# Causal attention between two feed-forward blocks: value products of two units put together in every second step of the attention phase

## The reference, cut to what matters

```
q = x @ w_q.T ; k, v = split(x @ w_kv.T)      # 16 heads of 32, one shared k and v
q, k = rotary(q), rotary(k)
attn = softmax(where(causal, q k^T, -max))     # per head 512 x 512, lower triangle
out  = attn @ v                                # the value product
x    = x + out @ w_proj.T + b_proj
```

## Time and profile before

| | us |
|---|---|
| median of 3 runs | 2837.68 |
| lowest and highest | 2837.28, 2841.86 |
| the profiled execution's own time | 2843.29 |
| its span in the trace | 2841.4 |
| TensorE busy in it | 2738.1 (96%) |
| VectorE, ScalarE, GpSimd busy | 1863.3, 1127.3, 284.3 |
| attention phase in the trace | about 1094 to 1746 |

### The profile page before, as it was taken

The page is one execution under the profiler, slowest core; times in us unless marked ns, Lnnn a source line. Parts: engine busy times, 40 slices in busy tenths (PEclk is TensorE's granted clock), DMA queues, the critical chain, the costliest instruction groups (busy, mean ns, idle before and its releaser), DMA issues. The chain is left out here.

```text
span 2841.4 us, 41676 instructions
## 1 busy us (share of the span) xinstructions
PE 2738.1 (96%) x15520; PEld 2198.9 (77%) x15520; DVE 1863.3 (66%) x3543; ACT 1127.3 (40%) x2400; POOL 284.3 (10%) x295
## 2 busy tenths in 40 slices
PE   7999999999999996899999997999999999999998
PEld 6888888888888884567777765888888888888887
DVE  5667656766676655777777765656766766676655
ACT  3323333323333321677777773332333333333331
POOL 0000000000000002344444421000000000000000
PEclk9999999999999997899999998999999999999999
DMA  3210311121121103000000003211121122203100
GB/s 118 98 51 21 128 45 44 61 89 45 45 78 63 48 4 119 1 9 31 28 28 31 16 16 123 85 45 45 60 89 49 48 79 82 68 17 104 45 15 30
DMA packets 65165, 156.48 MB, mean 55 GB/s; under 512 B 6881, under 2 KB 7137, under 8 KB 64737
## 3 DMA queue, kind: packets, MB, share of 16 engines
q1 hardware_dynamic: 64992, 154.17, 16.1%
HBM read 128.97 MB, written 25.17 MB: 54 GB/s over the span
## 5 line engine op out<-in xcount | busy, mean ns | idle before, releaser
L347 PE MATMUL bank<-xnt_h,wgu_h 128*128 128x512 f32 x2048 | 804.0, 393 | 10.3 <-issue 7.4
L347 PE MATMUL bank<-xnt_h,wgu_l 128*128 128x512 f32 x2048 | 799.4, 390 | 0.0
L347 PE MATMUL bank<-xnt_l,wgu_h 128*128 128x512 f32 x2048 | 799.3, 390 | 0.0
L504 DVE TENSOR_TENSOR h<-bank,sg 128x512 f32<-128x512 f32 x256 | 176.9, 691 | 601.4 <-PE bank L347 587.1
L347 PEld LDWEIGHTS bank<-xnt_h,wgu_h 128*128 128x128 f32 x2048 | 385.9, 188 | 91.8 <-issue 8.9
L347 PEld LDWEIGHTS bank<-xnt_h,wgu_l 128*128 128x128 f32 x2048 | 385.8, 188 | 80.7
L347 PEld LDWEIGHTS bank<-xnt_l,wgu_h 128*128 128x128 f32 x2048 | 386.0, 188 | 79.2
L443 ACT ACTIVATE mag<-h 128x512 f32<-128x512 f32 x256 | 162.2, 634 | 702.5 <-DVE h L504 702.5
L366 PE MATMUL bank<-wd_h,hs_h 128*128 128x512 f32 x1024 | 400.5, 391 | 9.1 <-DVE hs_l L539 9.1
L366 PE MATMUL bank<-wd_l,hs_h 128*128 128x512 f32 x1024 | 399.9, 390 | 0.0
L366 PE MATMUL bank<-wd_h,hs_l 128*128 128x512 f32 x1024 | 399.8, 390 | 0.0
(11 more groups left out here) (107 smaller groups left out, 3060.6 us busy)
## 6 DMA issues: line engine op xcount, KB each, us to landing
raw_gu<-in_w_gu SPq DMA_DIRECT2D x128, 512.0 KB, 4.9
raw_d<-in_w_d SPq DMA_DIRECT2D x128, 256.0 KB, 2.6
x_mid<-x_sb SPq DMA_DIRECT2D x64, 256.0 KB, 2.0
x_sb<-in_x SPq DMA_DIRECT2D x32, 256.0 KB, 4.9
x_sb<-x_mid SPq DMA_DIRECT2D x8, 1024.0 KB, 5.7
x_sb<-x_mid SPq DMA_DIRECT2D x32, 256.0 KB, 4.6
out<-x_sb SPq DMA_DIRECT2D x32, 256.0 KB, 2.1
probs<-in_w_q SPq DMA_DIRECT2D x1, 1024.0 KB, 5.4
```

Of the source, the lines that this page charges most:

```text
L347: last = pe.matmul(ps, w[:, r, kind, k], xs[:, b, k], start=(i == 0), stop=(i == 3 * KD - 1))
L504: v.tensor_tensor(h[:, r], bank[UP + r % 2][:, :], sg[:, r % 2], ALU.mult).then_inc(h_done, 1)
```

## The change

The step of TensorE no longer issues one value product each. Steps of odd row (1 and 3) issue none. Steps of even row issue two: that of unit K - 2 and then that of unit K - 1. So row 0's steps weigh rows 2 and 3 of the head group before, and row 2's steps weigh rows 0 and 1 of their own. After the last step both remaining units are weighed. `pt` keeps its size but is addressed by eight block places: row 0 uses place 7, row 1 places 5 and 6, row 2 places 0, 1 and 2, row 3 places 3, 4, 5 and 6. Nothing else in the program is different: the same matmuls, copies and waits are issued.

```diff
-    pt = place("pt", [P, 2, TT, HG, P], F32)
+    pt = place("pt", [P, 2 * TT, HG, P], F32)
...
+            PLACES = ((7,), (5, 6), (0, 1, 2), (3, 4, 5, 6))
...
                                 last = pe.matmul(outs[s * HD:(s + 1) * HD, i * P:(i + 1) * P], kvtok[:, B % 2, j, 1],
-                                                 pt[:, K % 2, j, s], start=(j == 0), stop=(j == i))
+                                                 pt[:, PLACES[i][j], s], start=(j == 0), stop=(j == i))
...
-                        if K > 0:
+                        if k % 2 == 0 and K > 0:
+                            weigh(K - 2)
                             weigh(K - 1)
                         if K + AHEAD < ALL:
                             scores(K + AHEAD)
...
                     for K in range(ALL):
                         step(K)
+                    weigh(ALL - 2)
                     weigh(ALL - 1)
...
-                        a.copy(pt[:, K % 2, j], bank_of["p", K, j][:, :].rearrange("p (s n) -> p s n", n=P)).then_inc(pt_scalar, 1)
+                        a.copy(pt[:, PLACES[row_of(K)][j]], bank_of["p", K, j][:, :].rearrange("p (s n) -> p s n", n=P)).then_inc(pt_scalar, 1)
...
-                        v.tensor_copy(pt[:, K % 2, j], bank_of["p", K, j][:, :].rearrange("p (s n) -> p s n", n=P)).then_inc(pt_vector, 1)
+                        v.tensor_copy(pt[:, PLACES[row_of(K)][j]], bank_of["p", K, j][:, :].rearrange("p (s n) -> p s n", n=P)).then_inc(pt_vector, 1)
```

## The result

The changed kernel is faster: median 2829.15 us of 7 runs (2826.25 to 2831.38) against 2837.68 before (7 runs, 2834.62 to 2842.28), a ratio of 0.9966 with a 95% interval of 0.9954 to 0.9977, that is 10 us less (7 to 13); the ratio is made from all the runs, and the two medians alone are 8.5 us apart. A second set of runs of the same kernel gave a median of 2828.81 and a ratio of 0.9961 (0.9947 to 0.9975). The forecast was 2820.8, 17 us less. The direction held. The wide range (2815 to 2830) held with 0.85 us to spare; the likeliest case's own range (2816 to 2827) did not hold, and 2829.15 lies in the range that the prediction had given to rival A.

What follows compares the result with a forecast made beforehand. TensorE's own order was taken to set the pace. Visits 8.8, mask waits 9.1 and k = 15 1.3, less 1.4 and 0.9, gave 16.9 us off the median 2837.7: 2820.8, range 2815 to 2830.

Steps and rivals of the forecast that it cites:

- rival A: VectorE's masks late in more steps, so the waits only move; 4 to 9 us saved, say 2831; chance 0.11.
- fewer visits: TensorE's value products: 64 visits instead of 128, 0.14 us saved at each of 63, 8.8 us less.
- Entry to the scores: Odd steps, scores directly behind transposes: priced the same as entry to value products, bounds 0.05 us either way in 63 steps.
- the wait at row 0: Scores S512 waiting for the masks of S384, 0.59 or 0.16 us each: all 9.1 us of waits go.
- k = 15: Batches 0 to 5, a transpose's 1.08 us wait for a bank: 0.22 more work under it, 1.3 us gained.
- list of covers: Check that `pt`, `pv_done`, the exponentials of S512 and ScalarE's slack stay safe with later products; no cost booked.
- the wait at k = 9: Row 1's step without W8: S128 comes 4.87 us after S512, a new wait of 0.03 for masks.
- a sign of being wrong: Odd steps showing scores that wait 0.3 us or more for masks would prove the forecast wrong.
- where VectorE bounds: k = 9, 13 of batch 0 and k = 1, 5 of batch 7: W8's 0.36 us returns nothing, 1.4 lost.
- B: No measurable change: entry to scores and waits inside the pair cost 6 us and A holds too; 2835; chance 0.05.
- C: More saved: entry to scores cheaper by 0.05 us and visits worth more; 21 to 24 us, 2815; chance 0.04.
- D: Slower: a stop makes TensorE's clock fall once per batch, 28 us paid less 17 saved; 2849; chance 0.06.

Runs made afterwards that it cites:

- both waits mended: Changed kernel with row 0's product in its own step at k = 1, 5 (batches 0 to 6), last two statistics at k = 6, 7; 2823.09 us.

## Why the prediction was right or wrong

**Right: fewer visits.** 0.14 for each saved visit, read from W8, W16 and W24, is what joining gave on its own (0.56 for four). Entry to the scores cost the same as entry to the value products, as the rows at the slower clock had it (at k = 1 0.39 us after the turns of k and v begin, with S128 behind them or with W8), and the second product's waits inside a group cost nothing: W56 is 1.67 to the next start, as worked out. The rule of the Trainium skill ("TensorEngine Tiling (Array Packing)", Key Properties), that a change of tiling mode drains the engine, agrees in sign; what a single change costs no run here isolates.

**Right: the wait at row 0.** The 0.59 and 0.16 us are gone, and S384 to S512 is 3.11 as worked out. It was the larger half of the gain: 0.84 of 1.40 with the visits left as they were.

**Right: k = 15.** 1.08 became 0.86, as summed.

**Right in part by luck: the number.** The saving came to 10 us where 17 were forecast, and the range held it because its upper end had been set to take in part of rival A. The step of the prediction that failed most is the next one.

**Wrong: what W8 covered.** The step "fewer visits" put "transposes, S" in place of "transposes, W, S" and priced entry alone. It did not ask which release W8's 0.36 us were hiding. At k = 1 and 5 the projection of a q ends ahead of it, and the bank of that q comes free later, after two operations of VectorE (1.4 us after the projection's end at k = 1). The prediction's list of covers names `pt`, `pv_done`, the exponentials and ScalarE, and leaves out the three banks that go round. It cost 0.26 + 0.23 us in seven batches, 3.4 us in all, the largest miss; the weight loader's two rows of waits above add up to 3.5.

**Wrong in size: the wait at k = 9.** The place and the mechanism were forecast, 0.03 us; it measured 0.27. That is just under the 0.3 that the prediction had named as a sign of being wrong. The working let the scaling of the output begin 0.02 ahead of S512; it begins 0.14 behind it. In the kernel before 0.02 ahead is seen at k = 4, where S512 itself stands waiting and the scaling follows the masks. Where the product's end alone sets it, at k = 0, the kernel before already had 0.13 behind:

```profile
1377.34 1.14 PE L915 MATMUL bank<-kt,qt 32*128 32x512 f32 x8
...
1377.47 0.69 DVE L1175 TENSOR_TENSOR att<-bank,rt 128x512 f32<-128x512 f32 x1 [2.38 <-PE bank L939]
```

The working also took 0.05 from the last mask to the next scores, where 0.14 was seen. In five batches the two are 1.2 us.

**Wrong, the other way: where VectorE bounds.** 1.4 us were booked as lost in batches 0 and 7, because row 2 was to pay for the block that row 1 gained nothing from. In batch 7 at the full clock the two orders end within 0.14 us (43.68 and 43.82). Here are row 2's step with rows 0 and 1 apart, and then the same step with them joined and both waits mended:

```profile
1665.31 0.50 PE L916 MATMUL bank<-kt,qt 32*128 32x128 f32 x8 [1.97 <-DVE nmax L1164]
...
1668.04 0.71 PE L916 MATMUL bank<-kt,qt 32*128 32x256 f32 x8 [0.19 <-DVE nmax L1164]
...
1662.80 0.50 PE L916 MATMUL bank<-kt,qt 32*128 32x128 f32 x8 [2.32 <-DVE nmax L1164]
...
1665.53 0.71 PE L916 MATMUL bank<-kt,qt 32*128 32x256 f32 x8
```

From S128 to S256 it is 2.73 us in both: apart, S256 waited for masks too, and the added block lies under that wait. Batch 0 was not settled, as the clock differs there from trace to trace.

The ledger: 16.9 forecast, less 3.4 and 1.2, plus some 0.8 (batch 7's half of the 1.4), is 13. The interval of the times allows 7 to 13. The first pair of traces shows 9.7 from k = 0 of batch 0 to k = 12 of batch 7. The pair taken again, in which batch 7 stood at 0.96 in both, shows 12.2 (568.5 and 556.3); most of the difference is batch 7, 48.05 us in the one trace of the changed kernel and 45.20 in the other.

**The rivals.** A, that waits only move, was half true: two new ones came, but one of them for a bank and not for masks, and neither took back the 9.1 us, since S512 waits no more at k = 0, 4, 8 and 12. Its number, 2831, was nearer to the 2829.15 than the forecast was. B fell. C fell: entry to S was not cheaper. D fell as put, since batches 1 to 5 stand at a clock of 1.00 throughout; but it pointed at a real thing, the clock in the last batch. The prediction said there that the change makes no stop longer, and that was wrong: with W8 gone from the step, the wait before S128 grew from 1.96 to 2.32 us in batch 7 and from 2.63 to 3.27 in batch 0. Its threshold, a stop near 2 us, was wrong as a rule: the mended kernel has the same stops of 2.32 us in batch 7 and no fall.

## What to carry to other kernels

When work moves out of a step, write down for that step every resource that the moved work was covering, the buffers that go round among them, and not only the semaphore that it issues or waits for: 0.36 us of matmuls were worth more as a cover than the visit that their removal saved. Put moved work under a wait that the timeline already shows; here that alone gave 0.84 us a batch, and joining groups 0.14 for each visit. Distances taken from a step with a wait in it need not be those of a step without one: here it was 0.02 ahead and 0.13 behind.

## What was not expected of the hardware

The granted clock of one and the same order of work differed between executions: 0.89 and 0.96 for the changed kernel's last batch, 48.05 and 45.20 us. A difference of 3 us between two single traces is not yet a difference between two kernels; in the steady batches, at a clock of 1.00, repeats agreed within 0.02 us and small changes could be told there that the whole times could not resolve.
